# Where the nine half-size expert tiles stand: spread among the last full tiles, or all behind them

## The reference

```python
logits = xf @ router_w
gate_vals, idx = jax.lax.top_k(logits, 2)
gates = jax.nn.softmax(gate_vals, axis=-1)
for e in range(8):
    h = jax.nn.relu(xf @ w1[e] + b1[e]) @ w2[e] + b2[e]      # 128 -> 512 -> 128
    y = layernorm(xf + h) * gamma[e] + beta[e]
    out = out + (gate of e) * y
```

## Time and profile before

| | us |
|---|---|
| median of 3 runs | 642.25 (635.12, 642.25, 642.63) |
| the profiled execution | 634.62 |
| its span, first to last instruction | 632.6 |

### The profile page before, as it was taken

How to read it: one execution, slowest core, us unless ns; L and a number is a source line. 1 busy time by engine, 2 the same in 40 slices (tenths; PEclk the granted TensorE clock), 3 DMA queues, 4 the chain that set the end, 5 groups by cost and what they waited for, 6 DMA issues and landing times.

```text
span 632.6 us, 15180 instructions
## 1 busy us (share of the span) xinstructions
PE 485.4 (77%) x4392; PEld 371.7 (59%) x4392; DVE 449.1 (71%) x1760; ACT 337.0 (53%) x791; POOL 311.7 (49%) x446
## 2 busy tenths in 40 slices
PE   4688777867866968878868788877899999997500
PEld 3455445545534545555435478777799999996500
DVE  6876667865665668767747668585788888886667
ACT  4466547654545647556635545433455565554444
POOL 2530222485553463675753776555555555554400
PEclk9989779895887889989768799889899999998855
DMA  5175735544255222133310475476798888888298
GB/s 155 43 198 141 187 110 126 109 84 132 57 167 130 76 72 61 43 101 95 104 35 11 142 254 167 161 217 181 223 301 254 281 266 264 273 259 266 71 349 249
DMA packets 77731, 101.47 MB, mean 160 GB/s; under 512 B 14334, under 2 KB 61729, under 8 KB 77650
## 3 DMA queue, kind: packets, MB, share of 16 engines
q1 hardware_dynamic: 70082, 87.05, 47.0%
q0 software_dynamic: 6416, 12.93, 5.8%
q10 hardware_dynamic: 1152, 0.52, 0.4%
HBM read 74.31 MB, written 32.28 MB: 168 GB/s over the span
## 4 chain that ended last, share of the span: by engine, by line
PE 36%; DVE 10%; issue 9%; SPq 8%; DMA 6%; another core or an unknown queue 6%; ACT 4%; POOL 2%; POOLq 0%; ACTq 0%; DVEq 0%
PE sbk L883 11%; PE avb L895 5%; PE mbk L895 5%; SPq L403 4%; PE avb L806 3%; PE avb L803 2%; DMA stack_d<-kq 2%; DMA stk<-stack_d 2%; PE sbk L788 2%; PE mbk L815 1%; SPq L418 1%; PE mbk L761 1%; PE mbk L873 1%; ACT pexs L621 1%
## 5 line engine op out<-in xcount | busy, mean ns | idle before, releaser
L1569 POOL DMA_INDIRECT expert_d<-pexs,dest x103 | 107.0, 1039 | 88.5 <-DVE pexs L1361 58.8
L1075 DVE TENSOR_REDUCE mx<-mbk 128x4 f32<-128x768 f32 x96 | 91.2, 950 | 66.1 <-PE mbk L761 46.1
L1555 POOL DMA_INDIRECT sorted_d<-pay,slot x96 | 96.4, 1004 | 41.1 <-issue 26.7
L580 ACT ACTIVATE pexs<-sbk 128x768 f32<-128x768 f32 x96 | 77.5, 807 | 46.9 <-PE sbk L788 35.0
L883 PE MATMUL sbk<-pexs,stk 128*128 128x256 f32 (+1 forms) x304 | 71.8, 381 | 6.4 <-ACT pexs L621 4.9
L621 ACT ACTIVATE pexs<-sbk,stk 128x256 f32<-128x256 f32 (+1 forms) x152 | 58.2, 459 | 21.2 <-PE sbk L883 15.7
L761 PE MATMUL mbk<-stk 48*64 48x192 f16 (+1 forms) x512 | 36.7, 273 | 37.8 <-DVE mx L1075 23.3
L883 PEld LDWEIGHTS sbk<-pexs,stk 128*128 128x128 f32 x304 | 54.7, 201 | 13.9 <-issue 6.2
L788 PE MATMUL sbk<-stk 49*64 49x192 f16 (+1 forms) x512 | 38.0, 279 | 20.8 <-ACT pexs L580 13.2
L615 ACT ACTIVATE pexs<-mbk 128x256 f32<-128x256 f32 (+1 forms) x56 | 20.6, 367 | 59.2 <-PE mbk L873 31.9
L761 PEld LDWEIGHTS mbk<-stk 48*64 48x64 f16 (+1 forms) x512 | 13.9, 105 | 61.7 <-issue 46.7
(11 more groups left out here) (237 smaller groups left out, 1136.5 us busy)
## 6 DMA issues: line engine op xcount, KB each, us to landing
stk<-pack_d SPq DMA_DIRECT2D x38, 706.5 KB
pexs<-pack_d SPq DMA_DIRECT2D x18, 706.5 KB
stk<-stack_d SPq DMA_DIRECT2D x64, 144.0 KB
xn<-sorted_d SPq DMA_DIRECT2D x47, 132.0 KB
stack_d<-kq SPq DMA_DIRECT2D x16, 384.0 KB
pack_d<-in_w SPq DMA_DIRECT2D x16, 256.0 KB
stack_d<-kq SPq DMA_DIRECT2D x16, 192.0 KB
stk<-expert_d SPq DMA_DIRECT2D x6, 384.0 KB, 6.2
```

The source lines that it names most:

```text
L580: act.activation(pex[p % 2][m][:, :, :], sbk[:, :, 0:COLS], ACT.Exp, scale=0.25).then_inc(a_pex, 1)
L1075: dve.tensor_reduce(dst, mbk[:, :, 0:COLS].rearrange("p h (c s) -> p h c s", c=2), AX.X, ALU.max).then_inc(d_mx, 1)
L1555: pool.indirect_dma_start(sorted_d[:, :], bass.IndirectOffsetOnAxis(ap=slot[p % 6][:, 2 * k + w:2 * k + w + 1], axis=0), pay[p % 6][:, k, ...
L1569: pool.indirect_dma_start(expert_d[:, :], bass.IndirectOffsetOnAxis(ap=dest[fin % 6][:, k:k + 1], axis=0), ye[fin % 4][:, k, :], None, bou ...
```

## The change

A tuple names the places of the half tiles in the order of the 56 tiles: 27, 31, 34, 38, 41, 45, 48, 52 and 55. All other places hold full tiles. `chunks(g)` now asks whether g is in that tuple. The columns of the plan stay where they are: `column(g)` maps a place to its column. The wait for the half tiles' columns (`plan_made` 3) stands on SyncE's queue ahead of tile 27 instead of ahead of tile 47. No instruction is added or removed; the number of tiles, the bytes of every transfer and all buffers stay.

```diff
+AT_HALF = (27, 31, 34, 38, 41, 45, 48, 52, 55)
+assert len(AT_HALF) == HALF
...
-    return 2 if g < FULL else 1
+    return 1 if g in AT_HALF else 2
+
+
+def column(g):
+
+    halves = sum(h < g for h in AT_HALF)
+    return FULL + halves if g in AT_HALF else g - halves
...
-                row = sp.value_load(plan[0:1, 0, g:g + 1], min_val=0, max_val=NE * CAP)
+                row = sp.value_load(plan[0:1, 0, column(g):column(g) + 1], min_val=0, max_val=NE * CAP)
...
-                e = sp.value_load(plan[0:1, 1, g:g + 1], min_val=0, max_val=NE - 1)
+                e = sp.value_load(plan[0:1, 1, column(g):column(g) + 1], min_val=0, max_val=NE - 1)
...
-                if g == FULL:
+                if g == AT_HALF[0]:
                     sp.wait_ge(plan_made, 3)
```

More of the change, by code:

```diff
@@ L58 @@
 EARLY, EARLY_PAIRS = 24, 12
-assert EARLY * G <= 2 * COLS * EARLY_PAIRS - NE * (G - 1)
+assert EARLY <= AT_HALF[0] and EARLY * G <= 2 * COLS * EARLY_PAIRS - NE * (G - 1)
 def after(eng, sem, p, per=1, n=None):
```

## The result

The changed kernel is slower, by under 1%: 639.34 us (median of 12 runs, 634.14 to 645.22) against 635.20 us of the kernel before (12 runs, 629.53 to 642.63). The ratio is 1.0087, with a 95% interval of 1.0054 to 1.0121. Forecast was 6 us less; it is 4.1 us more by the medians and 5.5 us by the ratio. A second set of runs on another chip gave 1.0052 (1.0006 to 1.0097). The ratios leave out executions of over 1.5% above the fastest of their kernel, so they differ from the ratios of the medians, and the traces of after_again and gated_spread are of such slower executions.

What follows compares the result with a forecast made beforehand. TensorE bounds full tiles, DMA loads starve the half tiles in the tail. Gain 6.4 - 0.5 = 5.9, say 6 us: 628.6 against 634.62 us, or 636 from the 642.25 median; range 627 to 642.

Steps and rivals of the forecast that it cites:

- TensorE without waits ends 8.2 us sooner: Matmuls at full clock, never waiting, from `up` of tile 46 would end the last `down` at 585.9 us.
- That TensorE then has no waits: Mixed stretch: transfers keep up at a DMA share of 0.93; remaining waits priced at 0.5 us, bounds 0 and 3.3.
- The first rival: Tail: its stop comes with any order, not from loads, and moves with the work; gain 0 to 2 us, 15%.
- The DMA rival: Mixed stretch: DMA engines become the bound, half tiles wait, 3.3 us of the gain go and 3.1 stay; 22%.
- the slow one: Mixed stretch: late rows starve TensorE at half tiles and its clock falls, some 5 us per place; slower, 5%.
- The tail's loss through loads: Old tail: a half tile needs 2.71 us of transfers for 1.90 us of matmuls, so nine in a row can't be fed.
- The end of the stage: Last finish at 590.2 us, 7.1 sooner, less 0.7 for GpSimd's extra scatters: 6.4 us gained.
- 0.1 us from TensorE to VectorE: Stage's end: time allowed between the end of `down` 54 and VectorE's sum of that tile.
- The transfers at large: Page against it: at 425 GB/s a half tile's transfers take 2.0 us, leaving the change nearly nothing to save.

Runs made afterwards that it cites:

- after_again: The changed kernel, unchanged, run again beside the kernel before on another chip: 633.69 us, ratio 1.0052.
- gated_spread: Changed order, but GpSimd issues a full tile's second scatter only once VectorE has begun the tile after the next: ratio 1.0076 to the kernel before.
- paced_spread2: Changed order plus a pause: GpSimd zeroes 128x384 unused numbers behind each scatter from tile 12 on; 628.83 us, ratio 0.9970 to the kernel before.
- paced_tail2: Old order (half tiles at 47 to 55) plus GpSimd's 128x384 zero-writing pause behind each scatter from tile 12 on: ratio 1.0011 to the kernel before.
- paced_mid: Changed order with GpSimd's 128x384 zero-writing pause behind the scatters of tiles 12 to 50 only: ratio 0.9942 to the kernel before.
- paced_short: Changed order with a shorter GpSimd pause, 128x96 numbers, behind each scatter from tile 12 on: ratio 1.0073 to the kernel before.

## Why the prediction was wrong, step by step

**The time.** The median of 639.34 us lies in the stated range of 627 to 642. That is luck: the range was made wide by runs of the kernel before 7.5 us apart, and no rival priced what happened. The direction was wrong.

**TensorE without waits ends 8.2 us sooner: right as a number.** The forecast puts the last `down` at 585.9 instead of 594.12, a stretch of 93.2 us. With the pause it is 93.37, twice. Bare, it is 102.45 and 99.13.

**"That TensorE then has no waits": the step that failed.** I priced what is left of waiting at 0.5 us, with 3.3 us as the upper bound, because I asked only whether the transfers could keep up. They can: paced_spread2 runs the mixed stretch at more than the 0.90 that I took for a possible limit.

```profile
500.00:520.00 20.00, 20.00 (x147) 19.02 (x146) 17.42 (x79) 12.54 (x38) 15.51 (x22) 1.00 0.93 298
520.00:540.00 20.00, 20.00 (x151) 19.17 (x150) 17.03 (x74) 12.40 (x38) 14.71 (x22) 1.00 0.91 298
```

The share of 0.93 which the working asked for is there in one window, and 0.91 in the next. What stopped the kernel were signals held back during dense scatters. Against the paced stretch they cost 5.8 us in after_again, on the same chip, and 9.1 in the profile of after, on another. In the latter 1.8 us are the clock: behind an idle of 2.16 us `up` takes 3.65 us, where the full-clock one takes 1.89. The granted clock from 574.4 to 578 us is 0.53, so it is the lower of the two levels.

```profile
574.41 3.65 PE L892 MATMUL sbk<-pexs,stk 128*128 128x256 f32 x8 [2.16 <-ACT pexs L630]
```

**The first rival had the mechanism and the wrong price.** "The tail's stop is not one of loads" got 15% for exactly the row that mattered, the releaser "remote", and I took it that such a stop moves with the work, at a gain of 0 to 2 us. It didn't move with the work, it multiplied: from one or two stops to seven, one for nearly each half tile that draws two pairs of scatters together. The evidence against it, "no such stop in the full steps", was true of TensorE's row only: VectorE and ScalarE already waited for late signals there, up to 1.4 us, as the line at 516.39 shows. The stops of 2 us should have led to the question of what the full steps have that the tail lacks: a pause of 2 us between pairs of scatters. I had priced GpSimd at the end only.

**The DMA rival was out, and the slow one was right only in its sign.** Loads were hardly late in the mixed stretch: TensorE waits for one 0.4 us in after, for two up to 0.5 us in after_again, for none in paced_spread2. The rival on the slow side expected late rows and lower clock; late signals did it.

**The tail's loss through loads: half right.** It is real, but shows only once the signals are free (paced_tail2: 98.28 against 93.37 us, 4.9 of the 8.2 us).

**The end of the stage.** Forecast from the last `down` to the last scatter: 6.25 us (590.2 + 1.25 + 0.7, less 585.9), against 4.45 before. Measured: 7.57. From the sum of tile 54 to that of 55 the forecast has 2.95 and the trace 2.94; from there to the last finish 2.14 and 2.15; then to the last scatter 1.95 and 1.99. The missing 1.3 us are in "0.1 us from TensorE to VectorE": `down` 54 ends at 598.34 and its sum starts at 599.76, 1.42 later, behind three dense scatters. In paced_mid, whose last tiles have no filler, it is 0.84. So the same kind of late signal made that term too small; in after_again it is 2.37 us late and the whole end 8.55.

**The transfers at large.** The forecast set the 425 GB/s of the Trainium skill (HBM Reference, section Specifications) against the 246 to 277 GB/s of the rows. Fewer stops raise the rate to 298 GB/s at a share of 0.93 and 308 at 0.95 (paced_tail2, 570 to 580 us); so the engines are nearly full at some 300. The Trainium skill's figure is for a core that streams alone; this mix of transfers doesn't come near it.

**Why the total lay where it did.** after minus before by the ruler is 4.2 and 3.0 us; the medians say 4.1 and 1.4. The stretch has 1.1 and -1.2 of it, the end 3.1 and 4.2. So the two errors play different parts: the held signals ate the 8.2 us that the stretch should have gained and left it about even, and what makes the kernel slower than before is the end, where 1.8 us of loss were forecast. The forecast by the same ruler was -5.9 with its 0.5 for waiting. With the pause the change gains 2.1 us by the ruler (paced_spread2 against paced_tail2, the end's loss taken off; 1.5 by the medians), but the intervals of the two ratios overlap, so the runs alone don't show it.

## What to carry to other kernels

A releaser that names no engine and no transfer is a finding, not noise, and a wait that names its producer can hide the same thing: compare the end of the producer's record with the start of all its readers, and look at what a third engine does in between. When an edit evens out one resource, count for every other engine how its work bunches in the new order, GpSimd's indirect DMAs first. A pause where there is slack can be worth more than any reordering.

## What the runs showed of the hardware

- While GpSimd issues four indirect scatters in a run, 1.27 to 1.33 us apart in their pairs, signals of PE to ScalarE arrive 1.6 to 3.1 us late (after, paced_short) and those to VectorE with them. In most stops that is 0.75 to 0.95 us behind the end of the last scatter; the one at 571.31 in after ends inside the run. At 1.57 us apart they arrive 0.04 to 0.14 us behind the producer on ScalarE (paced_spread2). What holds them is not shown.
- In the same runs VectorE's signal reaches ScalarE 0.04 us behind its record. SyncE still issues transfers there (in the changed kernel at 505.91 and 507.45 us), so that it is held as well is not shown.
- The Trainium skill (DMA: Bandwidth & Descriptors, section SWDGE vs HWDGE vs iDMA) says that transfers issued by SyncE and ScalarE are immune to the interference by which VectorE locks GpSimd out of its descriptor rings. No run here tests that; the effect here is another, in the other direction.
- One call's chip ran the kernel before in 593 us, those of the other calls in 631 to 638, and its three traces have no stop named remote. That it lacks this hold is likely but not shown: no bare kernel has a trace there.
